# Normalised x turned by 16 DMAs and VectorE's 32x32 transpose instead of by TensorE, one batch ahead

## The reference, cut to what matters

```
xn = layernorm(x) * scale + bias            # over the 512 features
q, k, v = xn @ Wq + bq, xn @ Wk + bk, xn @ Wv + bv
k, v masked; 16 heads in layer 0, 8 in layer 1
q = softmax(q) over a head's features;  k = softmax(k) over the 512 rows
att = k^T v per head;   y = q att
h = layernorm(y) * scale' * (1 + s(emb)) + ...   # a FiLM conditioning, (s, t) = silu(emb) @ W_emb + b
x = x + silu(h) @ W_out + b_out
```

## Time and profile before

| | us |
|---|---|
| median of 3 runs (989.14 to 989.24) | 989.16 |
| profiled execution: span of the trace | 987.8 |
| TensorE busy | 956.6 |
| VectorE busy | 613.5 |
| ScalarE busy | 419.1 |
| GpSimd busy | 284.7 |

### The profile page before, as it was taken

The page is one execution under the profiler, slowest core; times in us unless marked ns, Lnnn a source line. Parts: engine busy times, 40 slices in busy tenths (PEclk is TensorE's granted clock), DMA queues, the critical chain, the costliest instruction groups (busy, mean ns, idle before and its releaser), DMA issues.

```text
span 987.8 us, 14264 instructions
## 1 busy us (share of the span) xinstructions
PE 956.6 (97%) x5066; PEld 798.0 (81%) x5066; DVE 613.5 (62%) x1247; ACT 419.1 (42%) x643; POOL 284.7 (29%) x307
## 2 busy tenths in 40 slices
PE   4989999999999999999999999999999999999987
PEld 3758888888888888886688888888888888888876
DVE  5787655656566555757876656565655556565563
ACT  5536335343443524345463453335335343543522
POOL 2033421314242041422134313142421314242230
PEclk9999999999999999999999999999999999999998
DMA  7543020020302103031460300203020020302002
GB/s 230 221 139 128 1 108 20 5 122 0 127 0 79 49 0 127 0 128 43 128 234 1 114 26 26 104 0 127 0 108 19 16 111 0 127 0 110 18 1 85
DMA packets 19609, 71.21 MB, mean 72 GB/s; under 512 B 3392, under 2 KB 3448, under 8 KB 13440
## 3 DMA queue, kind: packets, MB, share of 16 engines
q1 hardware_dynamic: 19584, 70.88, 19.1%
HBM read 54.10 MB, written 16.78 MB: 72 GB/s over the span
## 4 chain that ended last, share of the span: by engine, by line
PE 91%; DVE 5%; issue 2%; POOL 1%; ACT 0%; POOLq 0%; SPq 0%; DVEq 0%; ACTq 0%
PE psum_w L368 52%; PE psum_k L368 18%; PE psum_k L592 5%; PE psum_k L554 5%; PE psum_t L582 3%; PE psum_t L432 3%; PE psum_t L419 3%; DVE w_low_k L739 1%; PE psum_t L527 1%; PE psum_t L396 1%; POOL q L1137 1%; DVE y L916 0%; DVE y L777 0%; DVE x_in L659 0%; PE psum_k L564 0%
## 5 line engine op out<-in xcount | busy, mean ns | idle before, releaser
L1083 POOL TENSOR_TENSOR xT_low<-xT,xT_high 128x512 fp32r<-128x512 f32 x60 | 77.3, 1288 | 239.6 <-ACT xT_high L980 238.2
L1075 POOL TENSOR_SCALAR x_var<-x_moments 128x4 f32<-128x4 f32 x16 | 3.7, 228 | 373.6 <-DVE x_moments L653 365.6
L1003 ACT ACTIVATE gate<-psum_t,film_shift,film_scale 128x512 f32<-128x512 f32 x64 | 49.7, 776 | 144.1 <-PE psum_t L432 114.0
L368 PE MATMUL psum_k<-w_high_k,xT_high 128*128 128x512 f32 x256 | 105.3, 411 | 0.5 <-DVE y L916 0.5
L368 PE MATMUL psum_w<-w_high_v,xT_high 128*128 128x512 f32 x256 | 103.7, 405 | 0.4 <-DVE emb_parts L823 0.4
L368 PE MATMUL psum_w<-w_high_q,xT_high 128*128 128x512 f32 x256 | 101.2, 395 | 0.0
L368 PE MATMUL psum_k<-w_high_k,xT_low 128*128 128x512 f32 x256 | 101.1, 395 | 0.0
L368 PE MATMUL psum_w<-w_high_v,xT_low 128*128 128x512 f32 x256 | 101.1, 395 | 0.0
L368 PE MATMUL psum_w<-w_low_q,xT_high 128*128 128x512 f32 x256 | 101.1, 395 | 0.0
L368 PE MATMUL psum_w<-w_high_q,xT_low 128*128 128x512 f32 x256 | 101.1, 395 | 0.0
L368 PE MATMUL psum_w<-w_low_v,xT_high 128*128 128x512 f32 x256 | 101.0, 395 | 0.0
(11 more groups left out here) (135 smaller groups left out, 1985.9 us busy)
## 6 DMA issues: line engine op xcount, KB each, us to landing
x_in<-x_between_layers SPq DMA_DIRECT2D x9, 1024.0 KB, 4.8
x_res<-in_x SPq DMA_DIRECT2D x8, 1024.0 KB, 6.8
x_between_layers<-x_res SPq DMA_DIRECT2D x8, 1024.0 KB, 3.9
x_in<-in_x SPq DMA_DIRECT2D x7, 1024.0 KB, 4.9
x_res<-x_between_layers SPq DMA_DIRECT2D x7, 1024.0 KB, 6.8
out_x<-x_res SPq DMA_DIRECT2D x7, 1024.0 KB, 3.9
raw_weights<-in_L_cond_film_emb_W SPq DMA_DIRECT2D x4, 1024.0 KB, 6.1
raw_weights<-in_L_cond_W_emb SPq DMA_DIRECT2D x4, 1024.0 KB, 5.1
```

The lines of the kernel that those rows point to most:

```text
L368: mm = pe.matmul(bank, lhs[:, c, rows_of_tile], rhs[w][:, c, :], start=(c == 0 and n == 0), stop=(c == CHUNKS - 1 and n == 2))
L1003: act.activation(gate[:, c % 2, :], psum_t[:, c % 2, :, :].rearrange("p t s -> p (t s)"), ACT.Silu, scale=film_scale[:, cond, c:c + 1].rea ...
L1083: pool.tensor_tensor(xT_low[:, c, :], xT[:, c % 2, :], xT_high[:, c, :], ALU.subtract)\
```

## The change

- `turn_x` is gone from the iterations; only batch 0 is still turned by TensorE (`turn_first_x`).
- `next_xn(i+1)` moves on VectorE from behind Q tile 3 to behind the maximum of Q tile 0 (before the bias of Q tile 1).
- SP gets `deal_x(i+1)`: it waits for the four `xn_ready`, then issues 16 DMAs from SBUF to SBUF, each of 32 partitions, 4 tiles and 128 contiguous features (64 KB in pieces of 512 B), from `x_in` to the new tile `x_quads`.
- VectorE gets `turn_next_x(i+1)` behind the last Q maximum: it waits for all 16 DMAs, then runs four 32x32-block transposes of 128x512 from `x_quads`, read with a stride of four elements, back into `x_in`. It stands ahead of the scaling of att.
- ScalarE's `scale_x(i+1)` moves from behind the four qT copies to ahead of them, and works in place in `x_in`. GpSimd's `split_x` reads `x_in`.
- The next load of x waits for `xT_low_ready` instead of `xT_psum`. The feature of partition p and chunk c is now 4p + c, so Q, K and V weights and the layer-norm scale and bias are loaded in that order; the latter by four DMAs of their own (`load_ln_params`).
- In iterations 0 and 7 some of the weight loads are issued behind the 16 DMAs (in iteration 0 all from FiLM piece 3 on, in iteration 7 the weights of layer 1).

```diff
 (VectorE)
+            def turn_next_x(i):
+                dve.wait_ge(x_dealt, 16 * QUADS * QUADS * i)
+                for c in range(CHUNKS):
+                    dve.transpose(x_turned_of(i)[:, c, :].rearrange("p (t j) -> p t j", j=QUAD),
+                                  x_quads[:, :, :, :].rearrange("p t b (f c) -> p c (t b) f", c=CHUNKS)[:, c])\
+                       .then_inc(x_turned_ready, 1)
...
                     if with_film and t == 0:
                         split_film(layer_film, 1)
+                    if with_next and t == 0:
+                        next_xn(i + 1)
                 if with_film:
                     copy_film_rows(layer_film, 0)
                     split_film(layer_film, 2)
                 if with_next:
-                    next_xn(i + 1)
+                    turn_next_x(i + 1)
 (SyncE)
+            def deal_x(i):
+                sp.wait_ge(xn_ready, TILES * (i + 1))
+                for at in range(QUADS):
+                    for b in range(QUADS):
+                        sp.dma_start(x_quads[at * QUAD:(at + 1) * QUAD, :, b, :],
+                                     x_in[b * QUAD:(b + 1) * QUAD, :, at * P:(at + 1) * P]).then_inc(x_dealt, 16)
...
+                sp.wait_ge(xT_low_ready, CHUNKS * (i + 1))
                 if with_next:
-                    sp.wait_ge(xT_psum, CHUNKS * (i + 1))
                     load_x(i + 1, 1 if fixed(i, LAST_0) else layer)
...
+                if with_next:
+                    deal_x(i + 1)
+                if fixed(i, 0):
+                    for n in range(RAW_BEFORE_0 + 3, RAW_IN_0):
+                        load_raw(n)
 (TensorE)
-                if with_next and not with_output:
-                    turn_x(i + 1, 0)
-                    turn_x(i + 1, 1)
                 attend(0)
                 attend(1)
-                if with_next:
-                    if with_output:
-                        turn_x(i + 1, 0)
-                        turn_x(i + 1, 1)
-                        out_projection(out_layer, i - 1, 3)
-                    turn_x(i + 1, 2)
+                if with_next and with_output:
+                    out_projection(out_layer, i - 1, 3)
                 attend(2)
-                if with_next:
-                    turn_x(i + 1, 3)
                 attend(3)
 (ScalarE)
+                if with_next:
+                    scale_x(i + 1, 1 if fixed(i, LAST_0) else layer)
                 for t in range(TILES):
                     act.wait_ge(qT_psum, TILES * i + t + 1)
                     act.copy(qT[:, t, :, :], psum_t[:, t % 2, :, :]).then_inc(qT_ready, 1)
...
-                if with_next:
-                    scale_x(i + 1, 1 if fixed(i, LAST_0) else layer)
```

More of the change, by code:

```diff
@@ L61 @@
 GROUP = 256
-PARAMS = (5 + 2) * CHUNKS
-LN_SCALE, LN_BIAS, BK, FILM_SCALE, FILM_BIAS, FILM_EMB_BIAS = (r * CHUNKS for r in range(6))
+QUADS, QUAD = 4, 32
+PARAMS = (3 + 2) * CHUNKS
+BK, FILM_SCALE, FILM_BIAS, FILM_EMB_BIAS = (r * CHUNKS for r in range(4))
+LN_SCALE, LN_BIAS = range(2)
 def build_program(nc, a, out):
@@ L113, in build_program, with x_turned_of @@
         x_rstd = sb("x_rstd", [P, TILES])
-        xT = sb("xT", [P, 2, SEQ])
+        x_quads = sb("x_quads", [P, TILES, QUADS, P])
+        def x_turned_of(i):
+            return x_quads[:, :, :, :].rearrange("p t b n -> p t (b n)") if fixed(i, 0) else x_in
         xT_high = sb("xT_high", [P, CHUNKS, SEQ], F32R)
@@ L267, in load_raw @@
                         part % 2 * EMB // 2:(part % 2 + 1) * EMB // 2, part // 2 * DIM:(part // 2 + 1) * DIM]
-                else:
-                    weights = key(layer, NAMES[layer][part])
-                sp.dma_start(slot, weights.rearrange("(c p) n -> p c n", p=P)).then_inc(raw_loaded[n % 2], 16)
+                    weights = weights.rearrange("(c p) n -> p c n", p=P)
+                elif part == O:
+                    weights = key(layer, NAMES[layer][part]).rearrange("(c p) n -> p c n", p=P)
+                else:
+                    weights = key(layer, NAMES[layer][part]).rearrange("(p c) n -> p c n", p=P)
+                sp.dma_start(slot, weights).then_inc(raw_loaded[n % 2], 16)
             def load_x(i, layer):
@@ L286, in load_params, with load_ln_params @@
                     at += n
+            def load_ln_params(layer):
+                for n, name in enumerate(LN_NAMES[layer]):
+                    sp.dma_start(ln_params[:, layer, n, :], a[name].rearrange("(p c) -> p c", p=P))\
+                      .then_inc(ln_params_loaded, 16)
+            def deal_x(i):
[4 more added lines that the diff above has]
+                                     x_in[b * QUAD:(b + 1) * QUAD, :, at * P:(at + 1) * P]).then_inc(x_dealt, 16)
             bias_v_row = bias_v[:, :, :].rearrange("p g n -> p (g n)")
@@ L325, in iteration @@
                 if fixed(i, LAST_0):
-                    for n in range(RAW_IN_0, RAW_IN_LAST_0):
+                    for n in range(RAW_IN_0, RAW_IN_0 + 2):
+                        load_raw(n)
[3 more added lines that the diff above has]
+                    for n in range(RAW_BEFORE_0 + 3, RAW_IN_0):
+                        load_raw(n)
+                if fixed(i, LAST_0):
+                    for n in range(RAW_IN_0 + 2, RAW_IN_LAST_0):
                         load_raw(n)
@@ L427, in turn_y @@
                 if c < 2:
-                    pe.wait_ge(xT_ready, CHUNKS * (min(j + 2, ITERS) if isinstance(j, int) else j + 2) - 1 + c)
+                    pe.wait_ge(qT_ready, TILES * j + c + 3)
                 else:
@@ L472, in _ @@
             for c in range(CHUNKS):
[L473 removed]
+                turn_first_x(c)
             def iteration(layer, i, with_output, with_next):
@@ L972, in scale_x @@
                 for c in range(CHUNKS):
[L973 to L978, removed]
+                    if fixed(i, 0):
+                        act.wait_ge(xT_psum, c + 1)
+                        turned = psum_t[:, c % 2, :, :].rearrange("p t s -> p (t s)")
+                    else:
+                        act.wait_ge(x_turned_ready, CHUNKS * (i - 1) + c + 1)
+                        turned = x_turned_of(i)[:, c, :]
+                    act.activation(x_turned_of(i)[:, c, :], turned,
+                                   ACT.Identity, scale=ln_params[:, layer, LN_SCALE, c:c + 1],
+                                   bias=ln_params[:, layer, LN_BIAS, c:c + 1]).then_inc(xT_ready, 1)
                     act.wait_ge(xT_ready, CHUNKS * i + c + 1)
-                    act.copy(xT_high[:, c, :], xT[:, c % 2, :]).then_inc(xT_high_ready, 1)
+                    act.copy(xT_high[:, c, :], x_turned_of(i)[:, c, :]).then_inc(xT_high_ready, 1)
             def preload_silu():
```

31 lines of the change are left out of this document (17 added, 14 removed).

## The result

The changed kernel takes 1166.91 us (median of 4 runs, 1166.3 to 1168.9) against 989.2 in the same job (989.14 to 991.0): 1.1794 times as long, 95% interval 1.1776 to 1.1811. Predicted were 1066 and a range of 1000 to 1105. The direction was right, the size was not: 178 us came instead of 77. The span of the profiled execution is 1167.1, 179.3 above that of before.

A forecast was written before the change was run, and what follows sets the result against it. TensorE, 97% busy, was taken to bound the kernel. New waits less 1.74 us of removed transposes gave 65.6 us in 13 iterations, plus 11 for iterations 0 and 7: 987.8 + 65.6 + 11, plus 1.4, 1066 us; range 1000 to 1105.

The forecast's parts named there:

- Step 3: The 16 DMAs issued by SP: 0.40 us per issue, 7.9 us to the last landing, bounds 6.0 to 11.2.
- Step 4: VectorE's four transposes after the last landing: pitch of 0.62 us, 2.5 us in all, bounds 1.9 to 5.0.
- The clock: Rival: TensorE's clock falls once per iteration after its waits, 1.65 us more each, 1087 us; chance 0.16.
- Step 5: VectorE's scaling of att takes turns with GpSimd, ending 3.2 us later than alone; residual tile 0 added at 669.9.
- Steps 1 and 2: Normalising x in turns with GpSimd takes 5.6 us; TensorE therefore loses 3.0 us waiting before Q tile 3.
- Iterations 0 and 7: Terms outside the regular iterations: +5 us (0 to 12) for iteration 0, +6 us (0 to 12) for iteration 7.
- Slow deal: Rival: the 16 DMAs take 11.2 instead of 7.9 us, +43, 1109 us; chance 0.08 shared with slow transposes.
- slow transposes: Rival: VectorE's transposes end 2.5 us later, +33, 1099 us; chance 0.08 shared with the slow deal.
- All hidden: Rival: VectorE keeps the port, no turns with GpSimd, all 1.74 us remain in 13 iterations, 969 us; chance 0.15.

The follow-up runs named there:

- two_queues: Changed kernel with eight of each batch's 16 DMAs issued by ScalarE and eight by SyncE: 1084.10 us, 1.0939.
- one_tile: Changed kernel with each of the 16 DMAs moving one of the four tiles only (output not the reference's): 1155.90 us, 1.1679.
- contig: Changed kernel with VectorE's transposes reading 32 adjacent elements instead of every fourth (output not the reference's): 1153.04 us, single run.
- xn_early: Kernel before with only the four normalising ops moved behind the maximum of Q tile 0, without DMAs or VectorE transposes: 1056.88 us, 1.0666.
- fill: Changed kernel with 48 unused TensorE transposes added before output tile 2, in layer 0 before turning att: 1158.03 us, 1.1694.
- both: Changed kernel; GpSimd's residual bias ahead of x's rstd, VectorE's transposes behind scaling att and residual tiles 0 and 1, scale_x behind qT copies: 983.70 us, 0.9938.
- best: `both` with normalising behind Q tile 1's maximum, FiLM piece 3 loaded ahead of the DMAs, iteration 0's transposes ahead of the mask maximum: 971.45 us, 0.9803.
- pool_first: Changed kernel with GpSimd adding the output bias to the residual ahead of the rstd of the next x: 1127.75 us, 1.1392.
- xn_early_fill: Kernel before with normalising behind Q tile 0's maximum, plus 28 unused TensorE transposes before Q tile 3: 1038.28 us, 1.0484.

## Why the prediction was wrong

The path was right, and so was each step's place. Iteration 10, against the working:

| step | predicted | measured | off by |
|---|---|---|---|
| 1 x normalised at (122.53 taken off) | 652.7 | 652.98 | +0.3 |
| 3 first issue to last landing | 7.9 | 11.7 | +3.8 |
| 4 four transposes | 2.5 | 4.1 | +1.6 |
| 5 from there until residual tile 0 is added | 6.8 | 5.3 | -1.5 |
| output tile 2 starts | 669.9 | 674.1 | +4.2 |
| from there to the next K | 10.0 | 12.3 | +2.3 |

5.0 + 4.2 + 2.3 = 11.5; the period grew from 57.77 to 69.30.

- **Step 3 is the one that failed, as a term mis-sized**: "I take 0.40", from issues of 0.45 and 0.31 that moved data between HBM and SBUF. These took 0.60, one every 0.643 us: 15 x 0.643 = 9.65, and 2.1 for the landing. 11.7 lies above even the upper bound of 11.2, which had doubled the landing (4.4) and kept the pitch at 0.45. The landing was right (1.9, 2.1); the pitch counts fifteen times and had the narrow bounds. two_queues shows that the number of issues in a row is what is paid, and one_tile that their size is not.
- **Step 4** was mis-sized by 1.6 us, inside its bounds (1.9 to 5.0). No row of before had the operation, and I took the price of one that reads adjacent elements, which was right for that (0.68, contig). The stride of four was in the diff. By the estimate from the figure of the Trainium skill, VectorE: DVE Perf Modes, "The three transpose paths", sixteen transposes of 128x128 bf16 would have been 5.0 us; measured were 4.1 for the same number of elements in float32.
- **The clock** was a rival at 0.16 and priced at 1.65 us per iteration, because the one gap that was read, of 4.95 us, put waits of 3.0 and 3.7 "at the edge". It belonged into the main case. The trace of before already had a fall at a shorter gap, in iteration 0: TensorE's row after it, with the idle time in brackets, and the window behind it.

```profile
66.00 0.61 PE L396 MATMUL psum_t<-w_high_o,emb_parts 128*16 128x512 f32 x1 [3.24 <-DVE w_low_o L739]
...
66.00:68.00 2.00, 2.00 (x5) 0.65 (x6) 1.97 (x5) 0.78 (x2) 0.00 (x0) 0.50 0.12 46
```

  In xn_early it fell at waits of 3.1 us in most iterations, so the two waits of the forecast would have been enough for it. Behind output tile 2's wait of 5.9 us it cost 2.3 in iteration 10; fill gave 2.05 back in the mean. It also falls at Q tile 3 after the wait of 3.1 us (0.69 in the window 776 to 778), but in the kernel after that costs nothing, as the chain runs past it through VectorE and SP; in xn_early, where Q tile 3 is on the path, it costs 1.3 us in the mean.
- **Step 5** was right in kind, and 1.3 us too dear: the turns cost 1.9, not 3.2. Of these 0.75 are L911, which I had not counted.
- **Steps 1 and 2** held: 5.56 us for 5.6. TensorE's wait was 3.1 for 3.0.
- **Iterations 0 and 7**: +11.0 and +12.3 for +5 and +6, within the 0 to 12 of iteration 0 and 0.3 above that of 7. In iteration 0 the chain goes through the issues of the deal, then the load of FiLM piece 3 behind them (5.4 us) and ScalarE's work on it, as the edit was read; iteration 7 has the same late deal as the others.

The range failed for a reason of its own. Slow deal, slow transposes and clock stood as rivals, one at a time, each with a chance: 1109, 1099, 1087. They add up. By my own prices all three together are 1066 + 43 + 33 + 21 = 1163, and 1166.9 was measured. That the two agree within 4 us is in part luck. Per iteration the three prices are too high together (7.5 us, where all steps together were off by 6.5, with step 5 against the others), and iterations 0 and 7 were 12 us dearer than their terms. But the point stands: the slow deal and the slow transposes both lengthen one wait in VectorE's queue, and the clock falls behind that wait, so the range should have held at least two at once.

All hidden, the rival that came out faster, has a time near those of `both` and `best`: 983.7 and 971.5 against its 969. But not by its mechanism. VectorE did not keep the port; the order of the lists had to be changed. Nor was its condition met, a last landing at or before 658.7: in iteration 10 of `both`, which begins 0.3 us before that of the kernel before, the last piece lands at 661.0. What decides is that the transposes end before something needs them, and their place in the list sets when that is.

## What to carry to other kernels

Before pricing a step on another engine, write down what is queued in order behind its wait: here the same slow deal costs nothing if the transposes stand behind the scaling of att (`both`), and 10 us per iteration if they stand ahead of it (`pool_first`). A count in a sum (fifteen pitches, four transposes) wants the widest bounds, from an operation of the same kind (source, partitions, stride), and errors that feed one queue belong into one range added up. A wait of 3 us or more that is expected on TensorE's own path is to be priced with the clock's fall, as part of the case and not as a rival to it: here it fell at ten of thirteen such waits in xn_early.

## What the runs showed of the hardware

- A DMA from SBUF to SBUF over 32 partitions takes 0.60 us to issue on SP (kernel after), 0.63 on ScalarE's queue (two_queues), and 0.59 when it moves 32 pieces of 512 B instead of 128 (one_tile); those of the earlier trace rows, from HBM, took 0.45 and 0.31.
- A 32x32-block transpose of 128x512 float32 on VectorE takes 0.68 us from adjacent elements (contig) and 1.07 with a stride of four (kernel after).
- L685 and L1153 in turns take 1.39 us a pair (kernel after); without L1153 beside it an L685 takes 0.6 (pool_first). An operation on 128x4 elements with two SBUF inputs takes 0.94 us instead of 0.19, as it waits for a GpSimd operation to end.
- The granted clock fell to 1.2 GHz at ten of thirteen TensorE gaps of 3.1 to 3.7 us in xn_early, and in the gaps of 4.7 to 7.9 us of the kernel after; it cost 1.3 us in the mean in the first and 2.0 to 2.3 in the second. Small transposes in the gap kept it up and gave 1.3 and 2.05 back (xn_early_fill, fill).
